# Self-attention on one core: the value products two double units behind their transposes, four buffers for turned probabilities, rotating value buffers

## What is computed

```python
HEADS, DHEAD = 20, 64                      # 20 heads of 64
xn = layer_norm(x, g1, be1)                # x: 4 x 512 x 160
q, k, v = xn @ wq1, xn @ wk1, xn @ wv1     # each 160 -> 1280, split into 20 heads
scores = einsum('bhnd,bhmd->bhnm', q, k) * DHEAD ** -0.5
attn = softmax(scores, axis=-1)            # 512 x 512 for each of 4 x 20 heads
out = einsum('bhnm,bhmd->bhnd', attn, v)
x = out.reshape(B, N, 1280) @ wo1 + bo1 + x
```

## Time and profile before

| what | value |
|---|---|
| median of 3 runs | 1038.58 us (1038.11 to 1039.63) |
| span of the profiled execution | 1036.7 us |
| PE busy | 981.3 us, 95% of the span |
| DVE busy | 690.3 us, 67% |
| ACT busy | 591.5 us, 57% |
| POOL busy | 380.1 us, 37% |
| mean granted TensorE clock | 0.993 of full speed |

### The profile page before, as it was taken

How to read it: one execution, slowest core, us unless ns; L and a number is a source line. 1 busy time by engine, 2 the same in 40 slices (tenths; PEclk the granted TensorE clock), 3 DMA queues, 4 the chain that set the end, 5 groups by cost and what they waited for, 6 DMA issues and landing times.

```text
span 1036.7 us, 17534 instructions
## 1 busy us (share of the span) xinstructions
PE 981.3 (95%) x6376; PEld 707.1 (68%) x6376; DVE 690.3 (67%) x1171; ACT 591.5 (57%) x1332; POOL 380.1 (37%) x493
## 2 busy tenths in 40 slices
PE   7999978999999999999999999999989999999998
PEld 4566666666667656667666667666647589999887
DVE  2767646677773776773676773776753889999563
ACT  2666634766763667763667763667753555455442
POOL 2576623434332344342344341343330024444220
PEclk9999999999999999999999999999999999999999
DMA  6400050000000000000000000000000340000000
GB/s 134 94 2 1 1 147 1 1 1 2 1 1 2 1 1 2 1 1 1 2 1 1 1 1 1 2 1 1 2 1 8 101 110 1 1 1 1 2 26 26
DMA packets 25370, 17.64 MB, mean 17 GB/s; under 512 B 8565, under 2 KB 24101, under 8 KB 25285
## 3 DMA queue, kind: packets, MB, share of 16 engines
q1 hardware_dynamic: 25285, 16.52, 6.6%
HBM read 11.26 MB, written 1.31 MB: 12 GB/s over the span
## 4 chain that ended last, share of the span: by engine, by line
PE 64%; DVE 10%; ACT 5%; issue 4%; POOL 1%; DMA 0%; SPq 0%; DVEq 0%; ACTq 0%; POOLq 0%
PE banks L409 13%; PE banks L396 12%; PE banks L382 11%; PE banks L416 4%; ACT sa_probs L499 3%; PE banks L224 3%; PE banks L227 2%; PE banks L226 2%; PE banks L225 2%; PE banks L1641 2%; PE banks L1933 2%; DVE sa_negmax L571 2%; DVE ca_top L1776 2%; DVE ca_probs L1781 1%; PE banks L232 1%
## 5 line engine op out<-in xcount | busy, mean ns | idle before, releaser
L639 POOL TENSOR_SCALAR sa_probs<-sa_probs,sa_inverse 128x512 f32<-128x512 f32 x320 | 217.7, 696 | 372.4 <-DVE sa_inverse L575 372.3
L499 ACT ACTIVATE sa_probs<-banks,sa_negmax 128x512 f32<-128x512 f32 x320 | 215.8, 685 | 163.5 <-DVE sa_negmax L571 163.4
L571 DVE TENSOR_REDUCE sa_negmax<-banks 128x2 f32<-128x1024 f32 x160 | 188.8, 1219 | 12.4 <-PE banks L382 9.7
L396 PEld LDWEIGHTS banks<-ident,sa_probs 128*128 128x128 f32 x1280 | 145.7, 141 | 55.6 <-issue 27.6
L396 PE MATMUL banks<-ident,sa_probs 128*128 128x128 f32 x1280 | 174.0, 277 | 10.0 <-ACT sa_turned L510 5.8
L580 DVE COPY sa_turned<-banks 128x512 f32<-128x512 f32 x160 | 110.2, 689 | 76.3 <-PE banks L396 76.3
L409 PE MATMUL banks<-sa_turned,sa_v 128*64 128x512 f32 x640 | 155.0, 605 | 0.0
L382 PE MATMUL banks<-sa_k_parts,sa_q_parts 64*128 64x512 f32 x960 | 134.9, 412 | 1.9 <-ACT sa_probs L499 1.9
L510 ACT COPY sa_turned<-banks 128x512 f32<-128x512 f32 x160 | 94.3, 590 | 30.6 <-PE banks L396 28.8
L382 PEld LDWEIGHTS banks<-sa_k_parts,sa_q_parts 64*128 64x128 f32 x960 | 85.2, 187 | 31.2 <-issue 14.4
L409 PEld LDWEIGHTS banks<-sa_turned,sa_v 128*64 128x64 f32 x640 | 38.7, 136 | 74.3 <-issue 73.0
(11 more groups left out here) (218 smaller groups left out, 1724.9 us busy)
## 6 DMA issues: line engine op xcount, KB each, us to landing
w_o<-in_L_xattn_wo SPq DMA_DIRECT2D x2, 800.0 KB, 9.2
out<-x SPq DMA_DIRECT2D x4, 320.0 KB, 2.4
w_q_t<-in_L_xattn_wq_t SPq DMA_DIRECT2D x1, 1120.0 KB, 10.4
fold_values<-ca_turned SPq DMA_DIRECT2D x5, 192.5 KB
x<-in_x SPq DMA_DIRECT2D x1, 960.0 KB, 5.8
fold_values<-ca_probs SPq DMA_DIRECT2D x4, 192.5 KB
w_q_t<-in_L_xattn_wq SPq DMA_DIRECT2D x1, 640.0 KB, 6.6
w_o<-in_L_xattn_wk SPq DMA_DIRECT2D x1, 640.0 KB, 10.0
```

Of the source, the lines that this page charges most:

```text
L396: last = pe.transpose(b_turn[e][:, q * P:(q + 1) * P], probs[:, j % 2, e, q, k * P:(k + 1) * P], ident[:])
L499: act.activation(probs[:, j % 2, e, q, :], b_scores[u % 2][:, e, :], ACT.Exp, bias=negmax[:, u % RING, e:e + 1], accum_out=total[:, u % RI ...
L571: dve.tensor_reduce(negmax[:, u % RING, :], b_scores[u % 2], AX_X, ALU.max, negate=True).then_inc(s_max.sem, 1)
L639: pool.tensor_scalar(probs[:, j % 2, e, q, :], probs[:, j % 2, e, q, :], inverse[:, u % RING, e:e + 1], 1.0, ALU.mult, ALU.mult).then_inc( ...
```

## The change

Three things change together. First, `pv` runs two double units behind the turning in place of one (`PV_LAG = 2`): in `d` TensorE does the units `2d - 4` and `2d - 3`, none in `d = 0` and `d = 1`, and four at the end of a batch. Second, the turned probabilities have four buffers in place of two, and a copy waits for the product four units back. Third, the values' buffers are dealt out in turn over all batches (`v_buffer`), and a buffer waits for the product of the two pairs that had it three turns before. With the later products, ScalarE's `copy_att` moves from even `d` to odd `d`.

```diff
     LEAD = 2
-    V_BUF = (0, 1, 2, 0, 1)
-    V_BEFORE = (3 - 5, 4 - 5, 2 - 5, 0, 1)
+    V_BUFS = 3
     RING = 8
+    TURN_RING = QT
+    PV_LAG = 2
...
-        turned = sb("turned", [P, 2, 2, S])
+        turned = sb("turned", [P, TURN_RING, 2, S])
...
-        s_evac = sig("turned_copied", NU, 2)
-        s_evac_act = sig("turned_copied_act", NU, 2)
+        s_evac = sig("turned_copied", NU, TURN_RING)
+        s_evac_act = sig("turned_copied_act", NU, TURN_RING)
...
+        def v_buffer(b, j):
+
+            return (b * NPAIR // 2 + j // 2) % V_BUFS
...
-                    last = pe.matmul(b_out[e * HD:(e + 1) * HD, :], v[:, V_BUF[j // 2], k, c:c + HD],
-                                     turned[:, u % 2, e, :], start=(k == 0), stop=(k == QT - 1))
+                    last = pe.matmul(b_out[e * HD:(e + 1) * HD, :], v[:, v_buffer(b, j), k, c:c + HD],
+                                     turned[:, u % TURN_RING, e, :], start=(k == 0), stop=(k == QT - 1))
...
-                    if d >= 1:
-                        pv(b, 2 * d - 2)
-                        pv(b, 2 * d - 1)
+                    if d >= PV_LAG:
+                        pv(b, 2 * (d - PV_LAG))
+                        pv(b, 2 * (d - PV_LAG) + 1)
...
-                pv(b, NU - 2)
-                pv(b, NU - 1)
+                for u in range(NU - 2 * PV_LAG, NU):
+                    pv(b, u)
...
-                act.wait_ge(s_pv.sem, s_pv.at(b, u - 2))
-                act.copy(turned[:, u % 2, 1, :], b_turn[1]).then_inc(s_evac_act.sem, 1)
+                act.wait_ge(s_pv.sem, s_pv.at(b, u - TURN_RING))
+                act.copy(turned[:, u % TURN_RING, 1, :], b_turn[1]).then_inc(s_evac_act.sem, 1)
...
-                    if d % 2 == 0 and d > 0:
-                        copy_att(b, d // 2 - 1)
+                    if d % 2 == 1 and d > PV_LAG:
+                        copy_att(b, (d - PV_LAG) // 2)
...
-                dve.wait_ge(s_pv.sem, s_pv.at(b, 2 * QT * (V_BEFORE[j // 2] + 1) - 1))
+                dve.wait_ge(s_pv.sem, s_pv.at(b, 2 * QT * (j // 2 - V_BUFS + 1) - 1))
...
-                dve.wait_ge(s_pv.sem, s_pv.at(b, u - 2))
-                dve.tensor_copy(turned[:, u % 2, 0, :], b_turn[0]).then_inc(s_evac.sem, 1)
+                dve.wait_ge(s_pv.sem, s_pv.at(b, u - TURN_RING))
+                dve.tensor_copy(turned[:, u % TURN_RING, 0, :], b_turn[0]).then_inc(s_evac.sem, 1)
```

More of the change, by code:

```diff
@@ L565, in copy_v @@
                 dve.wait_ge(s_v.sem, s_v.at(b, j))
-                dve.wait_ge(s_pv.sem, s_pv.at(b, 2 * QT * (V_BEFORE[j // 2] + 1) - 1))
-                dve.tensor_copy(v[:, V_BUF[j // 2], j % 2 * 2:j % 2 * 2 + 2, :].rearrange("p a c -> p (a c)"), bank).then_inc(s_vsb.sem, 1)
+                dve.wait_ge(s_pv.sem, s_pv.at(b, 2 * QT * (j // 2 - V_BUFS + 1) - 1))
+                dve.tensor_copy(v[:, v_buffer(b, j), j % 2 * 2:j % 2 * 2 + 2, :].rearrange("p a c -> p (a c)"), bank).then_inc(s_vsb.sem, 1)
             def maxima(b, u):
```

## The result

The changed kernel takes 1057.82 us (median of 4 runs, 1055.87 to 1060.24) against 1038.34 us before: a ratio of 1.0183, 95% interval 1.0164 to 1.0202. It is slower by 1.8%, as forecast (1059.6 us, range 1053 to 1067).

A forecast was written before the change was run, and what follows sets the result against it. TensorE was taken to set the pace, with ScalarE's chain beside it having little room. 6.5 + 7.8 + 7.5 - 0.8 = 21.0 us on a 1036.7 us span, plus 1.9 to the median, gave 1059.6 us, range 1053 to 1067.

The forecast's parts named there:

- What bounds the kernel: TensorE's back-to-back work sets the pace, 6.29 us per odd d; ScalarE runs beside it with 0.12 us of room.
- Step 1: ScalarE's attention copy moves to odd d, ahead of the turned copy, not hidden: 18 x 0.36 plus 16 x 0.49 us slower.
- Step 2: Value products leave d = 1 and stand bare at each batch's end: 7.5 us lost, 0.8 us won in d = 1.
- Step 3: Four turned buffers and the rotation of the value buffers: no cost and no gain.
- (a): Rival: TensorE's idling in d = 1 halves the clock in each batch, 6.8 us more, 1066.4 us; chance 0.12.
- (b): Rival: ScalarE's moved attention copy is hidden after all, only step 2 is left, 1045.3 us; chance 0.08.
- (c): Rival: faster, weight loads' idle ahead of products is a hidden copy wait, up to 27.4 us won, 1032.2 us; chance 0.05.

The follow-up runs named there:

- att_last: The kernel after, with ScalarE's attention copy behind both turned copies in odd double units instead of ahead of the first; 1044.78 us, ratio 1.0054 to before.
- extra_copy: The kernel before plus one unused 128x512 ScalarE copy in odd double units from d = 3, between exponentials and first turned copy; 1055.54 us, ratio 1.0151.
- mid_late: buffers_only with the order of between_all only in d = 7, 11, 13 and 15, all else as before; 1030.43 us, ratio 0.9915.
- buffers_only: The kernel after with PV_LAG = 1 and the attention copy in even d, keeping four turned buffers and rotating value buffers; 1038.55 us, ratio 0.9995.
- between_all: between_pe, plus ScalarE's first turned copy between its two exponentials and, in odd d, VectorE's ahead of its inverses; ratio 0.9984 to before.
- between_pe: buffers_only with TensorE making the value products between the two turnings of a double unit instead of ahead of both; ratio 1.0024 to before.

## Why the prediction was right

**What bounds the kernel** was right, and att_last and extra_copy show it from both sides: TensorE sets the pace of the odd double units, and ScalarE's chain from the maxima to its first turned copy runs beside it with only 0.12 us of room.

**Step 1**, 14.3 us: the row of d = 16 gave 6.65 us, and the odd double units measure 6.64 to 6.66. d = 7, 11, 13 and 15 grew from 7.44, 7.38, 7.30 and 7.40 to 7.93, 7.87, 7.78 and 7.88: 0.48 to 0.49 each. Only its trace in the list of waits was foreseen wrongly: TensorE's matmuls wait for ScalarE 21 times, not 34 to 40. The weight loads of the same turning have 39 such waits. The ends of matmuls are modelled in this profile, so a gap of a quarter microsecond ahead of one can disappear; the pitch and the weight loads show it.

**Step 2**, 7.5 less 0.8 us: two more units at the batch's end cost 3.58 - 1.87 = 1.71 us, not 1.87, so 6.8 us. That term of the sum was 0.6 us too large over the four batches. d = 1 fell to 6.16 us everywhere. From 6.29, 6.98, 7.31 and 6.28 that is 2.2 us and not 0.8.

**The difference of 3.6 us** between the two spans is mostly the clock, and so in part a matter of which execution was profiled; the forecast lies 1.8 us above the median. The two batch starts with a fallen clock in the execution before lasted 21.49 and 21.14 us and the one without 20.60; after, all three last 22.31. Less the 1.71 us of step 2 that is 0.89 + 0.54 = 1.4 us won, and 1.4 us more in the two d = 1 behind them, which the sum had taken as the kernel's own. (mid_late shows the same without the change: its execution had no fall there, and its three batch starts last 20.60 us and its d = 1 6.28 to 6.30.) Against it stand the 0.5 us of d = 15 and 0.8 us of d = 16 in the last batch, where the clock fell. 0.6 us is the same term of step 2, and 1.0 us lies ahead of the self-attention: its first scores start at 163.41 us after and 164.40 before, which the change doesn't touch. In the fourteen executions profiled here they start at 163.2 to 163.8 us where the granted clock fell once in the 20 us ahead of them, and at 164.1 to 165.2 where it fell twice. That is 3.1 of the 3.6; 0.3 us more lie behind the self-attention, and what is left I have not traced.

**Step 3** was right: buffers_only is at 0.9995.

**The rivals.** (a) did not come about in d = 1: TensorE is busy for 4.85 us there, where 4.42 were reckoned, and with it idle for about 1.3 of 6.2 us the granted clock stays at 1.00. But the clock did fall once, in d = 15, and the four runs of the kernel after had mean clocks from 0.995 to 0.990 and times from 1055.87 to 1060.24. A part of (a) may be in the median, which is 2 us above the profiled execution; where the clock fell in the other three executions is not known. In the profiled one it fell at another place than (a) had it. By the Trainium skill's "TensorE: Matmul & The Clock Gate", section "What's actually happening", idling TensorE halves its clock. The rows of d = 15 of the last batch agree: two waits of 0.96 and 1.12 us, then 0.50. The rows of d = 1, with 1.3 us idle, and of d = 15 of the second batch, with one wait of 1.12 us, stayed at 1.00, so not every idle stretch does it. (b) fell with the pitch of 6.65 us. (c) fell too: the idle time of the weight loads ahead of the products is 74.4 us after, 73.0 before.

## What to carry to other kernels

A buffer or a longer distance helps only where something waits for it; look for that wait by name first. Where several engines run hand-written orders side by side, a small copy that moves with another change can land in the one stretch that has no room, and a stretch of the same trace that already has that order tells its price in advance. Move work only in the stretches where the bottleneck engine waits: the reordering of three engines' streams won 0.2% when made in all twenty double units (between_all) and 0.85% when made in four of them (mid_late), of which the pitches account for 0.6%; TensorE's part of it alone, made in all, lost 0.2% (between_pe).

## What the runs showed of the hardware

- The same matmul blocks in another order take another time with no wait between them: 6.48 us for scores, turning, products, projection, turning, against 6.29 for scores, products, turning, projection, turning. A turning takes 0.85 us up to a projection and 1.02 us up to value products.
- Two ScalarE copies of 128x512 back to back start 0.46 to 0.48 us apart, though each lasts 0.60; with an SBUF source (extra_copy) it is 0.51.
- The granted clock of one and the same kernel differs between runs in steps: of the runs before that stood beside att_last, eight took 1037.96 to 1038.62 us at 0.992 to 0.993, seven 1040.21 to 1040.46 us at 0.990, and one 1042.24 us. A difference of 2 us in this kernel can be nothing but that.
